# A four-layer graph network on one core: the attention's gathered rows in one ring of 21 items with one softmax step per slot, and the last layer's radial network and layer norm for two items at once

## The reference, cut to what matters

```python
# layer 2: attention over the edges that arrive at a node
e = sum(Q[receiver] * K[sender]) * scale
w = exp(e - segment_max(e, receiver)[receiver])
attn = segment_sum(w[:, None] * V[sender], receiver) / segment_sum(w, receiver)
x = layernorm(x + (x + attn @ Wo))
# layer 4: messages weighted by a small "radial" network of the edge's length
h = silu(silu(emb @ mlp_w0 + b0) @ mlp_w1 + b1);  w = h @ mlp_w2 + b2
m0 = w0 * s;  m1 = w1 * s * Y1;  m2 = w2 * v;  m3 = w3 * (v . Y1) / sqrt(3)
x = layernorm(x + segment_sum([m0, m3, m1, m2], receivers) @ W_out / 16)
```

## Time and profile before

| what | value |
|---|---|
| median of 3 runs | 5631.95 us (5623.3 to 5632.62) |
| the profiled execution, its own time | 5625.35 us |
| its span in the profile | 5623.7 us |
| busy share of the span: PE, DVE, ACT, POOL | 59%, 63%, 54%, 65% |
| attention, from its first gather to the next stage's first gather | 2490.9 to 3214.0 us |
| last layer, from its first gather to the end of the span | 4252.1 to 5623.7 us |

### The profile page before, as it was taken

How to read it: one execution, slowest core, us unless ns; L and a number is a source line. 1 busy time by engine, 2 the same in 40 slices (tenths; PEclk the granted TensorE clock), 3 DMA queues, 4 the chain that set the end, 5 groups by cost and what they waited for, 6 DMA issues and landing times. The chain is left out here.

```text
span 5623.7 us, 74514 instructions
## 1 busy us (share of the span) xinstructions
PE 3333.1 (59%) x15856; PEld 2601.5 (46%) x15856; DVE 3545.2 (63%) x12659; ACT 3016.3 (54%) x7426; POOL 3641.2 (65%) x3635
## 2 busy tenths in 40 slices
PE   3536555356626662646666466679886666666664
PEld 3536555344414441545555354445554444444443
DVE  6686555578877774757888733347774555555554
ACT  0106666378848881864555433335554555555554
POOL 5767777677757773877555177767774555555554
PEclk9999999999968886987777688865567777777777
DMA  2337777678827772655555488866672111112111
GB/s 73 77 82 239 238 240 244 160 224 251 250 76 223 226 226 78 205 177 158 168 167 164 150 228 225 225 187 206 205 212 68 52 54 55 54 54 54 55 54 47
DMA packets 819909, 861.98 MB, mean 153 GB/s; under 512 B 159976, under 2 KB 593741, under 8 KB 819099
## 3 DMA queue, kind: packets, MB, share of 16 engines
q1 hardware_dynamic: 703528, 673.45, 38.6%
q0 software_dynamic: 112896, 179.36, 13.5%
q10 hardware_dynamic: 3314, 7.36, 0.4%
HBM read 494.56 MB, written 370.75 MB: 154 GB/s over the span
## 5 line engine op out<-in xcount | busy, mean ns | idle before, releaser
L2151 POOL DMA_INDIRECT out_dram<-mss_o,kept_scat_idx x392 | 389.8, 994 | 452.2 <-ACT mss_o L1433 349.7
L1592 POOL DMA_INDIRECT att_xs<-t_t,kept_idx_a x392 | 370.2, 944 | 259.6 <-ACT att_xw L1719 137.9
L1895 POOL DMA_INDIRECT gs_xs<-t_t,kept_idx_b x392 | 369.8, 943 | 232.5 <-issue 118.9
L1035 POOL DMA_INDIRECT t_alpha<-gsm_raw,gsm_edge_idx x392 | 386.0, 985 | 165.6 <-issue 118.6
L2159 POOL DMA_INDIRECT mss_xs<-t_x,kept_idx_a x392 | 375.9, 959 | 168.1 <-issue 117.6
L534 POOL DMA_INDIRECT sort_xd<-in_x_dram,kept_dst_idx x392 | 379.6, 968 | 140.3 <-issue 118.5
L2015 POOL DMA_INDIRECT gs_xs<-t_z,kept_idx_a x392 | 379.5, 968 | 140.2 <-issue 119.2
L1025 POOL DMA_INDIRECT gsm_raw<-t_al,kept_idx_b x392 | 379.2, 967 | 124.6 <-issue 118.9
L1227 PE MATMUL gsm_hp<-kept_w,gsm_zT 128*128 128x128 f32 x1568 | 256.2, 313 | 342.3 <-ACT gsm_zT L1093 342.0
L536 POOL DMA_INDIRECT sort_xs<-in_x_dram,kept_src_idx x392 | 378.6, 966 | 119.5 <-issue 118.6
L216 PE MATMUL gs_tp<-kept_ident,gs_xs 128*128 128x128 f32 x784 | 277.7, 371 | 251.0 <-DMA gs_xs<-t_t,kept_idx_b 151.5
(11 more groups left out here) (561 smaller groups left out, 12127.7 us busy)
## 6 DMA issues: line engine op xcount, KB each, us to landing
t_t<-sort_o SPq DMA_DIRECT2D x66, 792.0 KB
t_x<-gsm_o SPq DMA_DIRECT2D x196, 264.0 KB
sort_x<-in_x_dram SPq DMA_DIRECT2D x66, 768.0 KB
gsm_x<-t_t SPq DMA_DIRECT2D x196, 256.0 KB
t_z<-gsm_z SPq DMA_DIRECT2D x196, 256.0 KB
out_dram<-gsm_o SPq DMA_DIRECT2D x196, 256.0 KB, 3.0
t_t<-l_o SPq DMA_DIRECT2D x49, 528.0 KB, 3.1
att_own<-t_t SPq DMA_DIRECT2D x49, 528.0 KB
```

The source lines that it names most:

```text
L1035: pool.indirect_dma_start(T["alpha"], bass.IndirectOffsetOnAxis(edge_idx[:, c:c + 1], 0), raw[:, c, :], None).then_inc(scattered[u], 16)
L1592: pool.indirect_dma_start(xs[q % RING][:, j, :], None, T["t12"][0:EP + N], bass.IndirectOffsetOnAxis(K["idx_a"][:, c:c + 1], 0)).then_inc( ...
L1895: pool.indirect_dma_start(xs[u][:, j, :], None, T["t12"], bass.IndirectOffsetOnAxis(K["idx_b"][:, c:c + 1], 0)).then_inc(gathered[u], 16)
L2151: pool.indirect_dma_start(T["out"], bass.IndirectOffsetOnAxis(K["scat_idx"][:, c:c + 1], 0), o[u][:, j, :], None, bounds_check=N - 1, oob_ ...
```

## The change

In the attention the sixteen tiles of gathered rows become one tile with 21 places, so that the factors of seven items can be read by one instruction. The copy of the factors and the scaling per item go. One instruction per block scales 28 scores (`scale_dots`). Each of the softmax's steps gets a slot of its own, and the weights are used at lag 16 and not 12. The reciprocal of the sums is taken after they are turned. The norm is measured and scaled for four items at once (`QUAD`) and without statistics in PSUM. Own rows, results and applied norms go by one item and not two, and `hp` has two buffers.

In the last layer the slots are written out by `in_slots`. The radial network works on two items at once in one PSUM tile `rad`, and the norm is measured and scaled for two items. The order of the steps on each engine is another, and the scatter runs 18 positions behind the gather. The steps `turn_x`, `project`, `turn_sums`, `reduce`, `turn_back`, `scale_x`, `copy_x`, `copy_msg`, `messages`, `scan` and `keep` have the same instructions as before, with one counting semaphore in place of four.

```diff
-SCATTER_LAG = 15
+FINAL_LAG = 18
...
-RING = 16
-PAIRS = ITEMS // 2
+RING = 3 * BLOCK
+QUAD = 4
+QUADS = -(-ITEMS // QUAD)
 FIRST_STEP = BLOCK + 1
-WEIGHT_LAG = FIRST_STEP + 4
-assert BLOCKS * BLOCK == ITEMS and PAIRS * 2 == ITEMS
+WEIGHT_LAG = FIRST_STEP + 8
+MEASURE_LAG = WEIGHT_LAG + 3 + QUAD
+APPLY_LAG = MEASURE_LAG + 2
+assert BLOCKS * BLOCK == ITEMS
 
 
...
-        xs = [sb(f"xs{r}", [P, 4, ROW1]) for r in range(RING)]
+        xs = sb("xs", [P, RING, 4, ROW1])
...
         flags_loaded = [sem(f"flags_loaded{v}") for v in range(2)]
         turned, copied, multiplied, dotted, kept = sem("turned"), sem("copied"), sem("multiplied"), sem("dotted"), sem("kept")
         soft_v, soft_p, exped = sem("soft_v"), sem("soft_p"), sem("exped")
...
+            def load_own(q):
+                if q >= BUFS:
+                    sp.wait_ge(combined, q - BUFS + 1)
+                sp.dma_start(as_tile_rows(own[q % BUFS][:]), tile_rows(T["t12"][0:EP], q // BUFS, q % BUFS)).then_inc(own_loaded[q % BUFS], 16)
+
+            def store(q):
+                t, u = q // BUFS, q % BUFS
+                sp.wait_ge(applied, q + 1)
+                sp.dma_start(tile_rows(T["t12"][T12_Z:T12_Z + EP], t, u), as_tile_rows(o[u][:])).then_inc(stored[u], 16)
             in_slots((load, 0, 1, ITEMS), (load_flags, 3, BLOCK, BLOCKS), (load_goes, WEIGHT_LAG - 2, 1, ITEMS),
-                     (load_own, WEIGHT_LAG - 2, 2, PAIRS), (store, WEIGHT_LAG + 7, 2, PAIRS))
...
-                column_to_row(small[:, ROWS:2 * ROWS], rden[:]).then_inc(soft_p, 1)
-            pe.wait_ge(o_set, 3)
-            in_slots((turn_weights, FIRST_STEP + 4, BLOCK, BLOCKS), (turn_carried_tops, FIRST_STEP + 2, BLOCK, BLOCKS),
-                     (turn_sums, FIRST_STEP + 3, BLOCK, BLOCKS), (turn_scores, FIRST_STEP + 1, BLOCK, BLOCKS),
-                     (attend, WEIGHT_LAG + 2, 1, ITEMS), (multiply, 1, 1, ITEMS), (turn, 0, 1, ITEMS),
-                     (turn_weighted, WEIGHT_LAG, 1, ITEMS), (turn_tops, FIRST_STEP + 1, BLOCK, BLOCKS),
-                     (turn_carried_sums, FIRST_STEP + 3, BLOCK, BLOCKS))
+                column_to_row(small[:, ROWS:2 * ROWS], run[:]).then_inc(soft_p, 1)
+            pe.wait_ge(o_set, BUFS + 1)
+            in_slots((turn_scores, FIRST_STEP + 1, BLOCK, BLOCKS), (turn_tops, FIRST_STEP + 2, BLOCK, BLOCKS),
+                     (turn_carried_tops, FIRST_STEP + 3, BLOCK, BLOCKS), (turn_sums, FIRST_STEP + 5, BLOCK, BLOCKS),
+                     (turn_carried_sums, FIRST_STEP + 6, BLOCK, BLOCKS), (turn_weights, FIRST_STEP + 7, BLOCK, BLOCKS),
+                     (attend, WEIGHT_LAG + 2, 1, ITEMS), (multiply, 1, 1, ITEMS), (turn, 0, 1, ITEMS), (turn_weighted, WEIGHT_LAG, 1, ITEMS))
 
...
+            def root(k):
+                act.wait_ge(measured, k + 1)
+                act.activation(sd[k % 2][:], var[k % 2][:], ACT.Sqrt, bias=K["quarter_eps"][:, 0:1], scale=1.0 / D).then_inc(rooted, 1)
+
+            def apply(q):
+                k, base, u = q // QUAD, 4 * (q % QUAD), q % BUFS
+                act.wait_ge(scale_made, k + 1)
...
+            in_slots((weight, WEIGHT_LAG, 1, ITEMS), (copy, 0, 1, ITEMS), (root, MEASURE_LAG, QUAD, QUADS),
+                     (apply, APPLY_LAG, 1, ITEMS), (exponents, FIRST_STEP + 3, BLOCK, BLOCKS))
 
...
+            def ring_factors(b):
+                first = BLOCK * b % RING
+                return xs[:, first:first + BLOCK, :, D]
+
             def dot(q):
                 dve.wait_ge(multiplied, q + 1)
                 dve.wait_ge(gathered[q % RING], 64 * (q // RING) + 64)
-                rows = xs[q % RING]
-                for j in range(4):
-                    dt = dve.tensor_tensor_reduce(prod[q % 2][:, j, :], qp[q % 2][:, j, :], rows[:, j, 0:D], 1.0, 0.0, ALU.mult, ALU.add,
-                                                  four_scores[q % BUFS][:, j:j + 1])
+                for j in range(4):
...
-                dve.tensor_copy(kB[:, 4 * q:4 * q + 4], rows[:, :, D])
-                place = 4 * (q % BLOCK)
-                dve.tensor_tensor(block_scores[q // BLOCK % 2][:, place:place + 4], four_scores[q % BUFS][:], rows[:, :, D], ALU.mult).then_inc(kept, 1)
+
+            def scale_dots(b):
+                dve.wait_ge(dotted, BLOCK * (b + 1))
+                dve.tensor_tensor(block_scores[b % 2][:].rearrange("p (q j) -> p q j", j=4), block_dots[b % 2][:].rearrange("p (q j) -> p q j", j=4),
+                                  ring_factors(b), ALU.mult).then_inc(kept, 1)
 
...
-            def invert_sums(b):
+            def finish_sums(b):
                 dve.wait_ge(soft_p, P_STEPS * b + 5)
                 link(dve.tensor_copy(carried[:, 2:3], small[0:ROWS, 0:1]))
-                link(dve.scalar_tensor_tensor(out=run[:], in0=joined[:, 0, :], scalar=carried[:, 2:3], in1=run[:], op0=ALU.mult, op1=ALU.add))
-                dve.reciprocal(rden[:], run[:]).then_inc(soft_v, 1)
+                dve.scalar_tensor_tensor(out=run[:], in0=joined[:, 0, :], scalar=carried[:, 2:3], in1=run[:], op0=ALU.mult, op1=ALU.add).then_inc(soft_v, 1)
 
             def take_weights(b):
                 dve.wait_ge(soft_p, P_STEPS * b + 6)
                 cols = slice(b * ROWS, (b + 1) * ROWS)
-                dve.tensor_copy(rdB[:, cols], small[:, ROWS:2 * ROWS])
-                dve.tensor_tensor(wB[:, cols], small[:, 0:ROWS], kB[:, cols], ALU.mult).then_inc(soft_v, 1)
+                dve.reciprocal(rdB[:, cols], small[:, ROWS:2 * ROWS])
+                dve.tensor_tensor(wB[:, cols].rearrange("p (q j) -> p q j", j=4), small[:, 0:ROWS].rearrange("p (q j) -> p q j", j=4),
+                                  ring_factors(b), ALU.mult).then_inc(soft_v, 1)
 
...
+            def count(q):
+                k, base = q // QUAD, 4 * (q % QUAD)
+                dve.wait_ge(combined, q + 1)
+                for g in range(base, base + 4):
+                    bn = dve.bn_stats(stats[k % 2][:, g, :], y[k % 2][:, g, :])
+                bn.then_inc(counted, 1)
+
+            def measure(k):
+                v, wide = k % 2, slice(0, 4 * min(QUAD, ITEMS - QUAD * k))
+                dve.wait_ge(counted, min(QUAD * (k + 1), ITEMS))
...
-            in_slots((take_weights, FIRST_STEP + 4, BLOCK, BLOCKS), (scan_tops, FIRST_STEP + 1, BLOCK, BLOCKS),
-                     (shift, FIRST_STEP + 2, BLOCK, BLOCKS), (scan_row_sums, FIRST_STEP + 3, BLOCK, BLOCKS),
-                     (dot, 2, 1, ITEMS), (scan, WEIGHT_LAG + 1, 1, ITEMS), (combine, WEIGHT_LAG + 2, 1, ITEMS),
-                     (measure, WEIGHT_LAG + 3, 2, PAIRS), (scale, WEIGHT_LAG + 4, 2, PAIRS),
-                     (find_flags, FIRST_STEP, BLOCK, BLOCKS), (scan_row_tops, FIRST_STEP + 1, BLOCK, BLOCKS),
-                     (scan_sums, FIRST_STEP + 2, BLOCK, BLOCKS), (invert_sums, FIRST_STEP + 3, BLOCK, BLOCKS))
+            in_slots((dot, 2, 1, ITEMS), (scale_dots, FIRST_STEP, BLOCK, BLOCKS),
+                     (scan_row_tops, FIRST_STEP + 2, BLOCK, BLOCKS), (shift, FIRST_STEP + 3, BLOCK, BLOCKS),
+                     (scan_sums, FIRST_STEP + 4, BLOCK, BLOCKS), (scan_row_sums, FIRST_STEP + 5, BLOCK, BLOCKS),
+                     (finish_sums, FIRST_STEP + 6, BLOCK, BLOCKS), (take_weights, FIRST_STEP + 7, BLOCK, BLOCKS),
+                     (scan_tops, FIRST_STEP + 1, BLOCK, BLOCKS), (find_flags, FIRST_STEP, BLOCK, BLOCKS),
+                     (scan, WEIGHT_LAG + 1, 1, ITEMS), (combine, WEIGHT_LAG + 2, 1, ITEMS), (count, WEIGHT_LAG + 3, 1, ITEMS),
+                     (measure, MEASURE_LAG, QUAD, QUADS), (scale, MEASURE_LAG + 1, QUAD, QUADS))
     end_stage(nc, owned)
 
...
-            pipeline(sp, (load_y, 7))
+            for q in range(ITEMS):
+                if q >= 6:
+                    sp.wait_ge(applied, q - 5)
+                sp.dma_start(y[q // 2 % 3][:, 4 * (q % 2):4 * (q % 2) + 4, :], part_rows(T["x3"][0:EP], q // BUFS, q % BUFS)).then_inc(y_loaded[q // 2 % 3], 16)
+                if q % 2 == 1:
+                    sp.wait_ge(y_loaded[q // 2 % 3], 32 * (q // 6) + 32)
 
...
+            def scatter(q):
+                pool.wait_ge(applied, q + 1)
+                for j in range(4):
+                    c = 4 * q + j
+                    pool.indirect_dma_start(T["out"], bass.IndirectOffsetOnAxis(K["scat_idx"][:, c:c + 1], 0), o[q % BUFS][:, j, :], None,
+                                            bounds_check=N - 1, oob_is_err=False).then_inc(scattered[q % BUFS], 16)
+            for q in range(ITEMS + FINAL_LAG):
                 if q < ITEMS:
-                    t, u = q // BUFS, q % BUFS
-                    wait_item(pool, scaled, t, u, 4)
+                    if q >= BUFS:
+                        pool.wait_ge(scaled, q - BUFS + 1)
                     for j in range(4):
                         c = 4 * q + j
-                        pool.indirect_dma_start(xs[u][:, j, :], None, T["x3"],
-                                                bass.IndirectOffsetOnAxis(K["idx_a"][:, c:c + 1], 0)).then_inc(gathered[u], 16)
```

(53 more changed lines are left out.)

342 lines of the change are left out of this document (173 added, 169 removed).

## The result

The kernel after takes **5165.1 us** (median of 4 runs, 5164.1 to 5166.3), the kernel before 5632.3 in the same comparison: a ratio of 0.917, 95% interval 0.916 to 0.919. The forecast was 5187 us, in a range of 5130 to 5340.

The account below looks back on a forecast made before the run. The attention was taken as bound by DVE's work, the last layer by engines waiting for each other, then by POOL. 5625.35-107 (attention)-338 (last layer) = 5180 profiled, 6.6 under the median: 5187 us, range 5130 to 5340.

Parts of the forecast that it names:

- The sum of the parts: Attention: DVE's work per item after the change, added from its steps, 5.26 us, taken as a 5.4 us slot.
- 0.66 us of waits: Attention: DVE's waits per item for the root and for TensorE inside the softmax, expected to be hidden, 0.
- 0.1 for hand-overs: Attention: an allowance of some 0.1 us per item, raising the slot from 5.26 to 5.4.
- the 12 us: Attention: added to the last dot's time, 3016 to 3028, since the same working fell 15 us short for the kernel before.
- Rival C: Attention: the waits stay (ACT or SyncE late, softmax step not ready), 6.0 us a slot, +50, 5237; chance 0.12.
- POOL's own instruction: Last layer: POOL's four gathers and four scatters, 4 x (0.961+0.997) busy plus 8 x 0.30 between, 10.27 us a position.
- the ramp: Last layer: 18 positions of gathers before the first scatter, at least 90 us, taken as 100.
- Rival D: POOL's own instructions grow when DVE is denser, 784 x 0.20 = +157 us, 5344; chance 0.05.
- savings of the pairs: Last layer, ACT per slot: 1.28 us less table loads, 0.25 less SiLU, 0.15 less root, from 7.90 to 6.2.
- Rival B: Last layer: TensorE or the rounds between engines set the slot, say 11.8 us, +120, 5307; chance 0.20.
- E: Rival, last layer: PE stays at 1.2 GHz, +157 us there, less 107, so slower at 5682; chance 0.03.
- Profiled execution and median: Whole kernel: the profiled execution's own time lies 6.6 us under the median, lifting 5180 to 5187.

Follow-up runs that it names:

- soft_old_slots: The kernel after with the softmax's steps back in five slots, two or three steps in one slot, weights at lag 12: 5192.8 us (0.923).
- tables_per_slot: The kernel after with extra one-column Sqrt and Silu instructions in the last layer, so four table loads stand in a pair as before: 5171.4 us (0.919).
- new_orders_no_pairs: The kernel before with only its last layer's TensorE and ScalarE steps in the new order, radial network and norm still one per item: 5271.1 us (0.936).
- pe_order_old: The kernel after with TensorE's steps in the last layer back in the old order, ScalarE's order kept new: 5354.3 us (0.951).

## Why the prediction was right, point by point

**What bounds each stage: right.** The attention follows the work on DVE, the last layer was one round between engines and is now POOL's.

**Attention, the slot.** The sum of the parts was 5.26 us, and 5.26 is what the slot measures. (To the hundredth that is luck: 0.16 of it are waits that the sum had at 0, so its work on DVE was put 0.16 too high.) The reciprocal of 28 columns was put at 0.33 on the line between 8 and 128 columns: 0.326. Of the 0.66 us of waits that were to be hidden none is left (0.15 a slot for ScalarE's exponents is new). What failed are two terms that no row had given: the **0.1 for hand-overs**, and **the 12 us** added because the same working had fallen 15 us short for the kernel before. Without both: 2502.9+14 x 5.0+83 x 5.26 = 3009.5, and the last dot starts at 3009.4. (Of the 15, 3 are a slip: before, weighting starts at lag 12, so the gather pace holds for dots 0 to 10 and not 12, and 2548+87 x 6.67 = 3128 is 12 short. What the 12 were was not tested.) The last dot comes 18.6 us ahead of the forecast 3028, in a stage that began 4.8 us later than before, and the tail after it is 82.5 us in place of 78.7: 18.6+4.8-3.8 is the 20 us between -107 and -127.

**Rival C** (waits stay, 6.0 a slot, +50) did not come about, but soft_old_slots shows that its mechanism exists: with two or three steps in a slot it is 5.94 in 2700 to 3000 us, and (552.0-10 x 5.0)/87 = 5.77 over the whole stage.

**Last layer, the bound.** "So all lie under POOL's 10.27, and POOL becomes the bound" is right. The term that was mis-sized is **POOL's own instruction**: 999 and 1014 ns in place of 961 and 997, so 10.48 us a position, +17 over 80 positions. The 10 us kept for stalls were not needed, the ramp was 95 in place of 100, and the y load and scatter waits of others cost nothing. The sum also counts the gathers of position 18 twice, 5 us: they lie in the time before the first scatter, and again in the 80 positions behind it. That the stage comes to -339 against -338 is errors that cancel, not accuracy. Rival D had the direction of this (forecast +157 at full size, 0.20 us each; it was 0.02 to 0.04). What it had wrong is which instructions count: not any VectorE instruction, but of those in this stage mainly L2334, beside which one gather in eight begins. The Trainium skill, "SBUF — State Buffer", section "SBUF: two separate sides", has VectorE lock GpSimd out for a whole instruction in some modes. The trace agrees for L2334: a gather that begins beside it ends 0.81 to 0.86 us after it, and most DMAs begin elsewhere and take their usual time.

**Last layer, the reason.** The prediction named the order first and then added up the savings of the pairs: 1.28 us of table loads, 0.25 of SiLU, 0.15 of roots. They were real (ACT is busy for 514.0 us in 820/10.48 = 78.2 slots, 6.57 each in place of 7.90 and against a forecast of 6.2) and beside the new order worth nothing: tables_per_slot puts the loads back at +6 us, and new_orders_no_pairs has none of the savings and a shorter position. **The step that said what each edit brings was too coarse.** It showed only that all engines would be below POOL. It didn't ask which edit was needed for that, and the answer is: either.

**Rival B** (a round of 11.8, 5307) did not happen here, but pe_order_old shows it: 11.93. TensorE's clock rose from 0.75 to 0.90 with the long pauses gone, as the argument against E had it, and E fell by that. The Trainium skill, "TensorE: Matmul & The Clock Gate", section "Part 1: The HAM clock gate", releases the clock by sustained activity, and the trace agrees.

**Profiled execution and median.** The prediction put it 6.6 us below the median. Here the profiled execution took 5164.1, 1.0 below the median of 5165.1, so this term was 5.6 us too high. Together with the 20 of the attention, 1 of the last layer and 4.8 less for the stages ahead, that makes the 22 us between 5187 and 5165. The kernel before was profiled in an execution whose granted clock was 1.00 over the first 1000 us, where the kernel after had 0.65 and 0.50; whether that is what the 4.8 us are was not tested.

**Open:** a kernel with the new attention and the new order without pairs was not run. From the two runs it would be near 5271-128 = 5143 us, some 20 below the kernel after; that is an estimate. Open too is which part of the pairs' package speeds up the old order, and what the last 12 us ahead of the last dot are in the kernel before.
